# A four-layer graph network: the last layer's composition moved into PSUM, and empty second halves no longer gathered

## The chip, the cores and the metric

The kernel runs on one core of a Trainium2 chip. The metric is the device time of one execution in microseconds (us). Engines are named as in the profile: PE is TensorE (PEld its weight loads), DVE is VectorE, ACT is ScalarE, POOL is GpSimd and SP is SyncE; a name with a q is an engine's own instruction queue.

## The reference, cut to what matters

Four graph layers over 3125 nodes and 103125 edges, each behind a layer norm and a relu, and each added to x. The change touches the first layer (three hops) and the last:

```python
# layer 0, three times
h, t = agg[head], agg[tail]
att = sum((h @ q_w) * tanh(rel * t @ k_w), axis=1)
w = segment_softmax(att, head)
agg = segment_sum(w * rel * t, head) / count, normalised
# layer 3, once
comp = ent_emb[src] + rel_emb[rel_id]
score = sum(comp * ent_emb[dst], axis=-1)
norm = segment_softmax(score, dst)
neigh = segment_sum(comp * norm, dst)
return tanh(neigh @ neigh_w)
```

## The kernel before, in words

Nodes are sorted by degree and laid into 25 blocks of 128, one node to a partition. The edges of a block are laid out in slots: a body holds S = 8 slots for each of its 128 nodes, in two halves of H = 4 slots. A block has as many halves as its largest degree asks for, so its last body can have an empty second half. The plan in SBUF holds, for each block, the number of halves and the first body; with the reference's inputs the blocks have 15, 11, 11, then four times 10, six times 9, six times 8, four times 7 and two times 6 halves. That makes 116 bodies, and 13 blocks with an odd number of halves. Blank slots point at a blank row; the softmax gives them weight zero.

Two of the layers gather rows of a table in DRAM with one indirect DMA on POOL for each slot, 128 rows of 512 bytes at a time. Both use `PairStream`: `words` and `land` are double buffers, by the parity of the body. SP's `feed` loads a body's words, waits for the rows of each half (`rows_in`), passes them on (`rows_ready`, L877) and, after the first half of body n, passes the words of body n + 1 (`pass_words`, L864). POOL's `gather_all` waits for the words of body n and, for each half, for `rows_used`, then issues four gathers (L895); it does so for every body and for one blank body behind the last. So POOL gets the words of the next body only when the first half of the present one has landed.

In the first layer DVE makes a one-hot of the kinds (L1509, `kinds`), multiplies landed rows with relation rows (L1518), and sums and scores; PE and ACT work between. The first layer repeats this in three hops.

In the last layer (`composed_attention`), for body n inside the loop:

- DVE: `kinds(n + 3)` (L2359), `mark`, the eight score reductions of body n over `comp` in SBUF (L2403), the softmax steps of `soft.scores`, then for each half `compose(n + 1)` (L2379, landed rows plus the relation rows in PSUM) and `hots(n + 2)` (L2368, the one-hot for PE), then a wait for ACT's weighed rows and `soft.add` (L975 to L984).
- PE: `widen_kinds(n + 3)` (L2258, eight small matmuls that spread the kinds over the partitions), then `relations(n + 2)` (L2269), 48 bf16 matmuls for each half: 4 slots, 4 parts of the 474 relations, 3 bf16 terms.
- ACT: `move_line(n + 3)` (L2305: an activation table load, then a copy of 1024 columns), the exponentials (L960, L961) of body n, `weigh(n)` (L2317, eight), and last `keep(n + 1)` (L2312, two copies of 512 columns of `comp`).
- POOL: the gathers of body n + 2, which wait for `compose(n)` through `rows_used`.

One more place is read below for its durations alone: the graph convolution's second pass over the edges (L2046, `sums(1, ...)`), where TensorE multiplies f32 rows with 25 tiles of counts, six matmuls of 512 columns and one of 128 for each tile, 175 matmuls that the trace records as 350.

Each engine's order is the order of the code; there is no scheduler.

## Time and profile before

| | |
|---|---|
| median of 3 runs | 10402.22 us (10383.02 to 10405.49) |
| the profiled execution's own time | 10442.8 us |
| its span, first to last instruction | 10441.0 us |
| mean granted PE clock | 0.78 of full speed |
| busy share: PE, DVE, ACT, POOL | 65%, 73%, 56%, 66% |
| first layer, from its first one-hot to the end of hop three | 2142 to 5855 us |
| last layer, its loop over the bodies | 9013 to 10366 us |

The span is the time from the first instruction to the last on the core. The profiled execution is 40.6 us (0.4%) above the median of the timed runs. An engine's busy share is an average over stages with different limits, so the two touched stages are read apart.

### The profile page before, as it was taken

What the parts mean: (1) busy time and instruction counts of PE and PEld (TensorE: products, weight loads), DVE (VectorE), ACT (ScalarE), POOL (GpSimd) and SP (SyncE); (2) the same over time, 40 slices, a digit from 0 to 9 for tenths busy, and PEclk for the clock granted to TensorE, in tenths of its full rate; (3) what the DMA queues carried; (4) which work ended last, traced back from release to release, by engine and by line L of the source; (5) the groups of instructions that cost most, each with busy time, mean ns of one, the idle gap of its engine ahead of it and who ended that gap; (6) DMA issues with size and microseconds to landing.
All of it is one profiled execution on the core that took longest, in us unless ns stands there. A gap on an engine that the chain in (4) does not pass through costs nothing. (4 is left out here: it accounts for less than half of the span.)

```text
span 10441.0 us, 223670 instructions
## 1 busy us (share of the span) xinstructions
PE 6793.8 (65%) x64938; PEld 5513.0 (53%) x64939; DVE 7662.8 (73%) x21955; ACT 5833.8 (56%) x12496; POOL 6924.2 (66%) x5757
## 2 busy tenths in 40 slices
PE   3983974456665666656666487777777748466665
PEld 2883973345454455545555355555555523366655
DVE  9779764557777677767777699899989910577776
ACT  4224224446665566646666398889879900255544
POOL 0777764067776777767777489779869640566665
PEclk8555555677877788877878799999999979678777
DMA  0110119532322323223222211111111185222222
GB/s 23 54 43 22 57 38 139 184 48 53 53 53 46 51 53 53 52 45 51 53 53 53 44 51 57 51 46 57 57 39 57 57 140 208 47 47 47 46 45 44
DMA packets 421738, 630.49 MB, mean 60 GB/s; under 512 B 274855, under 2 KB 332033, under 8 KB 397929
## 3 DMA queue, kind: packets, MB, share of 16 engines
q0 software_dynamic: 192432, 385.10, 17.9%
q1 hardware_dynamic: 161808, 158.87, 5.9%
q10 hardware_dynamic: 67401, 85.32, 3.4%
q8 instruction: 50, 0.82, 0.0%
q14 instruction: 47, 0.39, 0.0%
HBM read 527.43 MB, written 103.02 MB: 60 GB/s over the span
## 5 line engine op out<-in xcount | busy, mean ns | idle before, releaser
L895 POOL DMA_INDIRECT l_land<-table,l_words x3744 | 3598.9, 961 | 1342.8 <-issue 1157.7
L1709 POOL DMA_INDIRECT ell<-gat_stage_pay,gat_stage_at x576 | 1675.0, 2908 | 175.5 <-issue 175.5
L1392 PE MATMUL left_product_ps<-k_w,messageT 128*128 128x128 f32 x5616 | 1046.7, 343 | 529.9 <-ACT messageT L1427 529.9
L1392 PEld LDWEIGHTS left_product_ps<-k_w,messageT 128*128 128x128 f32 x5616 | 883.0, 240 | 736.2 <-ACT messageT L1427 736.2
L2269 PE MATMUL rel_ps<-relation_parts,hot 128*128 128x128 bf16 x11328 | 823.1, 247 | 414.8 <-DVE hot L2368 414.8
L1806 ACT COPY gat_probT<-gat_ps 128x512 f32<-128x512 f32 (+1 forms) x2100 | 1018.7, 550 | 96.2 <-PE gat_ps L1749 83.4
L1386 PE MATMUL left_turned_ps<-ident,message 128*128 128x128 f32 x2808 | 563.1, 336 | 732.3 <-DVE message L1518 732.1
L244 POOL DMA_INDIRECT ell<-pay,position x816 | 840.2, 1030 | 292.5 <-issue 283.2
L2269 PEld LDWEIGHTS rel_ps<-relation_parts,hot 128*128 128x128 bf16 x11328 | 802.6, 114 | 436.4 <-DVE hot L2368 436.4
L1443 ACT ACTIVATE weighed<-kept,l_prob 128x128 f32 x2784 | 888.9, 391 | 59.1 <-ACT l_prob L961 59.0
L1386 PEld LDWEIGHTS left_turned_ps<-ident,message 128*128 128x128 f32 x2808 | 390.5, 174 | 832.6 <-DVE message L1518 829.4
L1749 PE MATMUL gat_ps<-ident,gat_logit 128*128 128x128 f32 x3750 | 600.7, 295 | 311.4 <-ACT gat_logit L1798 291.7
L295 PE MATMUL looked_ps<-count,loT_wide 128*128 (+1 forms) x3264 | 755.6, 384 | 48.4 <-issue 45.3
L1378 PE MATMUL rel_ps<-relation_parts,hotT 128*128 128x256 bf16 x4248 | 775.6, 334 | 2.0 <-ACT hotT L1422 2.0
L295 PEld LDWEIGHTS looked_ps<-count,loT_wide 128*128 128x128 f32 x3264 | 744.7, 333 | 57.2 <-issue 54.7
L1439 ACT ACTIVATE right<-left_product_ps 128x512 f32<-128x512 f32 x702 | 417.8, 595 | 636.8 <-DVE l_score L1579 363.6
L1755 PE MATMUL gat_ps<-gat_probT,h 128*32 128x128 f32 x15000 | 706.4, 282 | 2.4 <-issue 2.1
L1749 PE MATMUL gat_ps<-ident,work 128*128 128x128 f32 x3750 | 573.9, 284 | 180.3 <-ACT work L1798 159.9
L981 DVE TENSOR_REDUCE part<-weighed 128x128 f32<-128x1024 f32 x348 | 666.8, 1916 | 25.7
L1749 PEld LDWEIGHTS gat_ps<-ident,gat_logit 128*128 128x128 f32 x3750 | 430.1, 147 | 476.0 <-ACT gat_logit L1798 327.7
L353 ACT CAST loT_wide<-loT 128x512 f32<-128x512 bf16 x408 | 252.0, 618 | 700.9 <-PE looked_ps L299 675.0
L1579 DVE CUSTOM_DVE_ANT_0 product<-right,left_now 128x128 f32<-128x128 f32 x2784 | 623.1, 287 | 8.6
(334 smaller groups left out, 16136.3 us busy)
## 6 DMA issues: line engine op xcount, KB each, us to landing
gcn_edges<-counts SPq DMA_DIRECT2D x50, 1600.0 KB, 8.5
l_land<-table,l_words POOLq DMA_INDIRECT x3744
rows<-low_dram SPq DMA_DIRECT2D x34, 1536.0 KB
counts<-pair_turned_sb ACTq DMA_DIRECT2D x12, 3200.0 KB
logs<-pair_logs ACTq DMA_DIRECT2D x12, 3200.0 KB, 18.2
ell<-pay,position POOLq DMA_INDIRECT x816
ell<-gat_stage_pay,gat_stage_at POOLq DMA_INDIRECT x576
l_words<-ell SPq DMA_DIRECT2D x476, 8.0 KB
```

What stands on the lines that cost most here:

```text
L244: pool.indirect_dma_start(c.ells[0][:, :], bass.IndirectOffsetOnAxis(ap=position[:, 0, t:t + 1], axis=0), pay[:, t, :], None).then_inc(pla ...
L295: pe.matmul(looked_ps[r % HALVES][:, j, :], loT_wide[:, r % CAST, j, :], count[:, bass.ds(tile + j, 1), :].rearrange("p a n -> p (a n)"), ...
L895: pool.indirect_dma_start(self.land[:, p, s, :], None, table[:, :], bass.IndirectOffsetOnAxis(ap=self.words[:, p, s, 0:1], axis=0)).then_i ...
L1378: mm = pe.matmul(rel_ps[:, pair, :].rearrange("p s d -> p (s d)"), hotT[:, k * (H // 2) + j, :], parts[:, t, :, :].rearrange("p s d -> p ( ...
L1386: mm = pe.transpose(messageT_ps[:, k * H + j, :], message[:, k * H + j, :], c.ident[:, :])
L1392: mm = pe.matmul(right_ps[:, k * H + j, :], messageT[:, k, j, :], k_w[:, :], start=True, stop=True)
L1443: last = nc.scalar.activation(weighed[:, s, :], kept[:, bass.ds(n % 2, 1), s, :].rearrange("p a d -> p (a d)"), ACT.Copy, scale=soft.prob[ ...
L1709: pool.indirect_dma_start(c.ells[1][:, :], bass.IndirectOffsetOnAxis(ap=stage_at[n % 2][:, t:t + 1], axis=0), stage_pay[n % 2][:, t, :], N ...
L1749: mm = pe.transpose(ps[:, q % 4, r * P:(r + 1) * P], logit[t % 2][:, j * P:(j + 1) * P], c.ident[:, :])
L1755: mm = pe.matmul(ps[C * r:C * (r + 1), 4 + t % 2, 0:P], xs[:, 4 * q + r, t * C:(t + 1) * C], probT[:, q % 4 * 4 + r, :], start=(q == 0), s ...
L1806: nc.scalar.copy(probT[:, q % 4 * 4:q % 4 * 4 + rows_of(q), :].rearrange("p r d -> p (r d)"), ps[:, q % 4, 0:rows_of(q) * P]).then_inc(mov ...
L2269: mm = pe.matmul(rel_ps[:, k * H + s, :], hot[:, k, g, s, :], parts[:, g, t, :], start=(g == 0 and t == 0), stop=(g == PARTS - 1 and t == 2))
```

## The change

**The stream.** `gather_all` and `feed` now walk the plan block by block (`each_body`). POOL issues the four gathers of a second half only where the body has one, counted by `seconds`, whose own parity chooses the semaphore; it does not gather the blank body behind the last. SP waits for the second half only where there is one, and signals `rows_ready` in any case. The parity of a body is now told by two `If` blocks (`by_parity`) and no longer by an unrolled pair. The landing buffers' second halves are set to zero once for each layer. Two new functions, `read_plan` and `gather_by_plan`, are called by nothing.

**The last layer.** `comp` and `rel3_ps` are gone; two PSUM tiles `comp3_ps0` and `comp3_ps1` (two banks each) take turns by parity. For each half PE adds the landed rows with one f32 matmul of 512 columns against the identity, and the 48 relation matmuls accumulate on top. DVE's scores read PSUM; ACT's `keep` copies from PSUM and now stands before the exponentials; DVE's two additions are gone, and DVE's scores wait for ACT's copies of that body.

```diff
 class PairStream:
     def open(self, v):
+        self.nc.vector.memset(self.land[:, :, H:S, :], 0.0)
+        v.drain()
+    def each_body(self, eng, visit):
+        with eng.Fori(0, self.z.blocks) as b:
+            many, whole, first = self.block(eng, b)
+            seconds = self.second(eng, b)
+            with eng.Fori(0, many) as i:
+                visit(eng.snap((first + i).with_bounds(min_val=0, max_val=self.z.bodies - 1)), i < whole, seconds + i)
+
+    def by_parity(self, eng, n, visit):
+        with eng.If((n & 1) < 1):
+            visit(0)
+        with eng.If((n & 1) > 0):
+            visit(1)
 # feed, for each body
+            self.by_parity(sp, n, first_half)
+            self.pass_words(sp, base + n + 1)
+            s = hop * all_seconds + seconds
+            with sp.If(has_second):
+                self.by_parity(sp, sp.snap(s), lambda q: stand(sp, self.sp_turns, self.rows_in[q][1],
+                                                               (s >> 1) * (16 * H) + 16 * H))
+            sp.sem_inc(self.rows_ready[1], 1)
+            self.by_parity(sp, n, lambda p: go_on(n, p))
 # gather_all, for each body
+            def both(p):
+                stand(pool, self.turns, self.words_ready, hop * (bodies + 2) + n + 1)
+
+                stand(pool, self.turns, self.rows_used[0], hop * bodies + n + 1)
+                half(p, 0, self.rows_in[p][0])
+                with pool.If(has_second):
+                    stand(pool, self.turns, self.rows_used[1], hop * bodies + n + 1)
+                    self.by_parity(pool, pool.snap(s), lambda q: half(p, 1, self.rows_in[q][1]))
 # last layer, PE
+                    pe.wait_ge(stream.rows_ready[k], m + 1)
                     pe.wait_ge(hot_ready[k], m + 1)
-                    pe.wait_ge(comp_ready[k], m + 2)
+                    if not first:
+                        pe.wait_ge(scored, m + (-1))
+                        stand(pe, pe_turns, kept_ready[k], m + (-1))
+                    def into(p):
+                        pe.matmul(comp_ps[p][:, k * H:(k + 1) * H, :].rearrange("p s d -> p (s d)"), c.ident[:, :],
+                                  stream.landed(m, k).rearrange("p s d -> p (s d)"),
+                                  start=True, stop=False).then_inc(stream.rows_used[k], 1)
 # last layer, ACT's loop
                     move_line(i + 3)
+                    for k in range(HALVES):
+                        keep(act.snap(i + 1), k)
                     soft.exponentials(act, i)
                     act.wait_ge(soft.prob_ready, i + 1)
                     for k in range(HALVES):
                         weigh(i, k)
-                    for k in range(HALVES):
-                        keep(i + 1, k)
 # last layer, DVE
-                V.tensor_tensor(comp[:, half, :], stream.landed(n, k), rel_ps[:, half, :],
-                                ALU.add).then_inc(comp_ready[k], 1)
+                            last = V.tensor_tensor_reduce(product[:, s, :], comp_ps[p][:, s, :], h_now[:, :], op0=ALU.mult,
+                                                          op1=ALU.add, scale=1.0, scalar=0.0, accum_out=soft.score[:, s, :])
```

How the instructions stand. ACT in the last layer's loop, before: from the copy of the widened kinds to the first weighed slot.

```order
L2305 ACT_TABLE_LOAD
L2305 COPY kind_line<-line_ps 128x1024
L2287 ISA
L2287 DMA kind3<-ell1 128x16
L959 REGISTER_ALU
L960 ACTIVATE l3_keep<-l3_drop 128x1
L961 ACTIVATE l3_prob<-l3_score 128x8
L2317 ISA
L2317 ACTIVATE weighed3<-kept3,l3_prob 128x128
```

ACT with the change, from the first copy of a composed half (after the same table load, copy of kinds and DMA) to the exponentials. Of the four copies two run, by parity:

```order
L2400 COPY kept3<-comp3_ps0 128x512
L862 UNCONDITIONAL_BRANCH
L864 COMPARE_AND_BRANCH
L2400 COPY kept3<-comp3_ps1 128x512
L864 UNCONDITIONAL_BRANCH
L862 COMPARE_AND_BRANCH
L2400 COPY kept3<-comp3_ps0 128x512
L862 UNCONDITIONAL_BRANCH
L864 COMPARE_AND_BRANCH
L2400 COPY kept3<-comp3_ps1 128x512
L864 UNCONDITIONAL_BRANCH
L1033 ACTIVATE l3_keep<-l3_drop 128x1
```

The two copies of 512 columns stood behind the eight `weighed3` rows and now stand ahead of `l3_keep` and `l3_prob`.

PE in the last layer's loop, before: the widened kinds and both halves' relation matmuls.

```order
L2278 ISA
L2258 MATMUL line_ps<-ident_b,kind_b 128x128 x8
L2264 REGISTER_ALU
L2269 MATMUL rel3_ps<-relation_parts3,hot3 128x128 x96
L2278 REGISTER_ALU
L2278 COMPARE_AND_BRANCH
```

PE with the change, from the widened kinds to the first half's end; the second half repeats the pattern:

```order
L2333 MATMUL line_ps<-ident_b,kind_b 128x128 x8
L2339 REGISTER_ALU
L2342 REGISTER_ALU
L862 REGISTER_ALU x2
L862 COMPARE_AND_BRANCH
L2346 ISA
L2346 MATMUL comp3_ps0<-l3_land,ident 128x512
L2352 MATMUL comp3_ps0<-relation_parts3,hot3 128x128 x48
L862 UNCONDITIONAL_BRANCH
L864 COMPARE_AND_BRANCH
```

A 512-column f32 matmul with the identity stands ahead of each 48, and each half is inside a branch by parity.

POOL in the first layer, with the change: one body of even parity in the loop. Before, a body was two waits on semaphores and eight gathers in a row.

```order
L44 ISA x2
L917 DMA l0_land<-table,l0_words 128x128 x4
L929 REGISTER_ALU x2
L929 COMPARE_AND_BRANCH
L862 ISA
L862 REGISTER_ALU
L862 COMPARE_AND_BRANCH
L917 DMA l0_land<-table,l0_words 128x128 x4
L862 UNCONDITIONAL_BRANCH
L864 COMPARE_AND_BRANCH
L917 DMA l0_land<-table,l0_words 128x128 x4
L864 UNCONDITIONAL_BRANCH
```

The second four gathers stand inside two branches, and the block's two table words are read ahead of the loop.

## Rows read from the trace of the kernel before

**Rows 1.** Busy us by engine in two stretches, instructions in brackets, granted clock, DMA share, GB/s

```profile
2142.20:5855.00 3712.80, 2326.01 (x14191) 1863.61 (x14192) 2747.10 (x12158) 2289.26 (x5942) 2740.90 (x2853) 0.79 0.29 51
9012.80:10365.60 1352.80, 866.61 (x12016) 839.00 (x12016) 1066.20 (x4938) 687.31 (x1611) 890.72 (x926) 0.79 0.27 46
```

**Rows 2.** Groups by line, last layer's loop: busy, mean ns, idle before and releaser

```profile
L895 POOL DMA_INDIRECT l_land<-table,l_words x926 | 891.3, 963 | 454.0 <-issue 274.7 <-DVE comp L2379 170.0 <-SPq L864 9.2
...
L2403 DVE CUSTOM_DVE_ANT_0 l_product<-comp,h_now 128x128 f32<-128x128 f32 x920 | 204.7, 285 | 0.0
```

**Rows 3.** Timeline of two bodies, last layer: start, length, engine, line, idle before

```profile
9735.45 0.17 DVE L2359 TENSOR_SCALAR kind_b<-kind 128x8 bf16<-128x8 int32 x1 [0.85 <-issue]
...
9735.96 0.61 PE L2258 MATMUL line_ps<-ident_b,kind_b 128*128 128x128 bf16 x8
...
9740.54 8.08 PE L2269 MATMUL rel_ps<-relation_parts,hot 128*128 128x128 bf16 x96 [3.97 <-DVE hot L2368]
...
9745.85 0.17 DVE L2359 TENSOR_SCALAR kind_b<-kind 128x8 bf16<-128x8 int32 x1 [0.85 <-issue]
...
9748.45 0.61 PE L2258 MATMUL line_ps<-ident_b,kind_b 128*128 128x128 bf16 x8
...
9749.32 1.28 ACT L2305 ACT_TABLE_LOAD   x1 [6.34 <-issue]
...
9751.04 5.53 PE L2269 MATMUL rel_ps<-relation_parts,hot 128*128 128x128 bf16 x96 [1.97 <-DVE hot L2368]
...
9751.52 0.21 ACT L960 ACTIVATE l_keep<-l_drop 128x1 f32<-128x1 f32 x1
...
9754.35 1.12 ACT L2312 COPY kept<-comp 128x512 f32 x2
9754.55 0.15 DVE L975 COPY l_top_now<-l_top_new 128x1 f32<-128x1 f32 x1 [1.92 <-ACT weighed L2317]
...
9758.31 0.17 DVE L2359 TENSOR_SCALAR kind_b<-kind 128x8 bf16<-128x8 int32 x1 [0.85 <-issue]
```

**Rows 4.** Waits, last layer: total us, times, longest

```profile
ACT L2305 <- PE line_ps L2258: 586.1, 107, 7.6
```

**Rows 5.** Timeline of TensorE in the graph convolution

```profile
8731.61 136.53 PE L2046 MATMUL gcn_ps<-gcn_edges,work 128*128 128x512 f32 x350 [40.52 <-issue]
```

**Rows 6.** The same stretch, columns as in group 1

```profile
8732.00:8868.00 136.00, 136.00 (x350) 63.05 (x349) 0.00 (x0) 0.00 (x0) 0.00 (x0) 0.99 0.70 253
```

**Rows 7.** Groups by line, one hop of the first layer

```profile
L895 POOL DMA_INDIRECT l_land<-table,l_words x934 | 896.2, 960 | 291.7 <-issue 289.2 <-SPq L864 2.1 <-DVE message L1518 0.3
```

**Rows 8.** Waits, first layer's three hops

```profile
DVE hot L1509 <- SPq L864: 421.8, 273, 8.5
...
POOL l_land L895 <- DVE message L1518: 0.3, 1, 0.3
```

**Rows 9.** Timeline around one end of a half's gathers, first layer

```profile
2632.55 0.98 POOL L895 DMA_INDIRECT l_land<-table,l_words  x1 [0.30 <-issue]
...
2635.91 0.69 DVE L1509 TENSOR_TENSOR hot<-iota_row,l_words 128x512 bf16<-128x512 f32 x1 [1.36 <-SPq L864]
...
2638.97 0.94 POOL L895 DMA_INDIRECT l_land<-table,l_words  x1 [0.30 <-issue]
```

**Rows 10.** Timeline of a POOL wake, last layer

```profile
9703.58 0.69 DVE L2379 TENSOR_TENSOR comp<-l_land,rel_ps 128x512 f32<-128x512 f32 x1 [0.19 <-issue]
...
9705.06 1.07 POOL L895 DMA_INDIRECT l_land<-table,l_words  x1 [2.59 <-DVE comp L2379]
```

**Rows 11.** DVE's waits in a middle stretch of hop one

```profile
DVE hot L1509 <- SPq L864: 76.2, 61, 4.2
```

**Rows 12.** The same in its last stretch

```profile
DVE hot L1509 <- SPq L864: 9.5, 6, 4.5
```

**Rows 13.** Timeline of the last layer's start

```profile
9006.11 0.69 DVE L2379 TENSOR_TENSOR comp<-l_land,rel_ps 128x512 f32<-128x512 f32 x1 [27.34 <-SPq L877]
...
9017.83 0.32 DVE L2359 TENSOR_SCALAR kind_b<-kind 128x8 bf16<-128x8 int32 x1 [4.58 <-DMA kind<-ell]
```

More of the change, by code:

```diff
@@ L871, in feed, with go_on @@
         self.load_words(sp, 1, 1)
-        def step(n, j, p):
-            for h in range(HALVES):
-                stand(sp, self.sp_turns, self.rows_in[p][h],
-                      (hop * self.of_parity(bodies, p) + j) * (16 * H) + 16 * H)
-                sp.sem_inc(self.rows_ready[h], 1)
-                if not h:
-                    self.pass_words(sp, base + n + 1)
+        def go_on(n, p):
             if kinds_done:
@@ L885, in feed @@
+        self.each_body(sp, step)
+        for h in range(HALVES):
+            sp.sem_inc(self.rows_ready[h], 1)
+        self.pass_words(sp, base + bodies)
+        last = sp.snap(bodies + (-1))
+        self.by_parity(sp, last, lambda p: go_on(last, p))
         self.pass_words(sp, base + bodies + 1)
     def gather_all(self, pool, hop, bodies, table):
[L889 to L897 removed]
@@ L899, in gather_all, with half, step @@
-        self.in_pairs(pool, bodies, step)
+        all_seconds = self.all_second(pool)
+        def half(p, h, landed):
+            for s in range(h * H, (h + 1) * H):
+                pool.indirect_dma_start(
+                    self.land[:, p, s, :], None, table[:, :],
+                    bass.IndirectOffsetOnAxis(ap=self.words[:, p, s, 0:1], axis=0)).then_inc(landed, 16)
+        def step(n, has_second, seconds):
+            s = hop * all_seconds + seconds
+            def both(p):
[5 more added lines that the diff above has]
+                    self.by_parity(pool, pool.snap(s), lambda q: half(p, 1, self.rows_in[q][1]))
+            self.by_parity(pool, n, both)
@@ new lines, in gather_all, with read_plan, gather_by_plan, half @@
+        self.each_body(pool, step)
+    def read_plan(self, pool):
+        return [pool.value_load(self.plan[0:1, b:b + 1], min_val=1, max_val=(1 << 31) - 1)
+                for b in range(self.z.blocks)]
+    def gather_by_plan(self, pool, hop, bodies, table, words):
+        most = self.z.bodies
+        def half(p, h, landed):
+            for s in range(h * H, (h + 1) * H):
+                pool.indirect_dma_start(
+                    self.land[:, p, s, :], None, table[:, :],
+                    bass.IndirectOffsetOnAxis(ap=self.words[:, p, s, 0:1], axis=0)).then_inc(landed, 16)
+        seconds = hop * self.all_second(pool)
+        for b, word in enumerate(words):
+            halves = word & ((1 << HALF_BITS) - 1)
+            many = pool.snap(((halves + 1) >> 1).with_bounds(min_val=1, max_val=most))
+            whole = pool.snap((halves >> 1).with_bounds(min_val=0, max_val=most))
+            first = pool.snap((word >> HALF_BITS).with_bounds(min_val=0, max_val=most))
+            s0 = pool.snap(seconds)
+            with pool.Fori(0, many) as i:
+                n = pool.snap(first + i)
+                def both(p):
+                    stand(pool, self.turns, self.words_ready, hop * (bodies + 2) + n + 1)
+                    stand(pool, self.turns, self.rows_used[0], hop * bodies + n + 1)
+                    half(p, 0, self.rows_in[p][0])
+                    with pool.If(i < whole):
+                        stand(pool, self.turns, self.rows_used[1], hop * bodies + n + 1)
+                        self.by_parity(pool, pool.snap(s0 + i), lambda q: half(p, 1, self.rows_in[q][1]))
+                self.by_parity(pool, n, both)
+            seconds = s0 + whole
```

85 lines of the change are left out of this document (41 added, 44 removed).

## The prediction

> **What bounds the kernel now.** Only two stages change, so I read each by itself: first the busy time of every engine in each stretch, then the groups by line, then the waits, and last the timeline of single bodies. The last layer's waits are small pieces that repeat, and only the timeline shows how they join.
>
> The first layer's three hops take 3713 us and POOL is busy for 2741 of them, no more than DVE [rows 1]. But a gather of 960 ns is followed by idle time that nothing in the profile ends ("issue"). With it one gather costs (896.2 + 291.7) / 934 = 1.27 us, and eight make 10.2 us, the whole pace of a body; POOL waited for DVE once, for 0.3 us [rows 7, 8]. DVE waits for the words 273 times, 421.8 us in all [rows 8]. So this layer is bound by POOL's gathers.
>
> The last layer is not. Its 116 bodies take 1352.8 us [rows 1], 11.66 each, and POOL waits for DVE's additions for 170 us [rows 2]. The timeline shows a short body of 10.40 us (K = 9735.45 to 9745.85, K being the start of the kinds) and a long one of 12.46 us (to 9758.31) [rows 3]. Both end by the same chain: line matmuls, 0.87 us later ACT's table load, 2.20 later the exponentials, 3.03 later DVE's L975, 3.76 later the next K, together 9.86 us. In the short body the line matmuls start at K + 0.51, and 0.51 + 9.86 = 10.37. In the long one they start at K + 2.60, because the relation matmuls of the body before began at its K + 5.09 and took 8.08 us; 2.60 + 9.86 = 12.46. The next batch took 5.53 us, was over before the next K, and so the next body is short again [rows 3]. ACT's waits agree: 586.1 us for the line matmuls, 107 times [rows 4]. What a body waits for last is PE's batch and then ACT's chain. DVE's 74 to 79% busy is no bound.
>
> **The stream, first layer.** 13 blocks have an odd number of halves; each drops four gathers in each hop: 39 bodies, 4 × 1.27 = 5.08 us of POOL's time each [rows 7]. Not all of it is won. SP passes the next body's words only when the first half has landed. In a whole body four more gathers cover that, in an odd one nothing does. From the start of a first half's last gather to the release of DVE, which SP's same turn brings, is 2635.91 − 2632.55 = 3.36 us [rows 9]. POOL then needs about 0.8 us to wake, as behind DVE's addition (9704.27 to 9705.06) [rows 10]. So 4.2 us pass where 6.42 (to 2638.97) pass now [rows 9], and an odd body wins 2.2 us, not 5.08.
>
> DVE must be able to follow. In the middle of a hop it waits 76.2 us over 61 waits, 1.25 each; in the last stretch, where the blocks of 7 halves lie, 9.5 us over 810 and 220 us [rows 11, 12]. So nine blocks win 2.2 and the four of 7 halves about 0.4: 3 × (19.8 + 1.6) = 64, rounded down for a first body here and there: **−62 us**. Bounds: −85 if DVE keeps up everywhere; −20 if each saved gap returns as a DVE wait. The new `If`s, table words and branches of POOL I cost at nothing: its sequencer runs ahead, since the 0.30 us before a gather is the same at a new body [rows 9]. If that cover failed, see the last rival. The blank body's gathers stood behind the last real ones and ended nothing; the memset is below 2 us. Second halves dropped in the last layer win nothing, since POOL waits there [rows 2].
>
> **The last layer.** Three edits touch the 9.86 us chain or the batch ahead of it.
>
> PE gets two f32 matmuls of 512 columns. The nearest row is the graph convolution: 136.53 us at a granted clock of 0.99 for 25 tiles, 5.46 us for six matmuls of 512 and one of 128 columns, each recorded twice [rows 5, 6]; 5.46 / 6.25 = 0.87 us for a matmul of 512. Two take 1.7 us at 2.4 GHz, and twice that, 3.4 us, at 1.2 GHz. The first batch of a pair takes 8.08 us against the other's 5.53 and so begins at the lower level; the mean granted clock is 0.79 [rows 1, 3]. I take +2.15 us: one half's at 2.4 GHz with part of the other's at 1.2. The start of the batch stays at K + 5.09: the one-hot comes 0.6 us sooner without the first addition, and three more waits and a branch stand before the batch.
>
> The Trainium skill ("TensorE: Matmul & The Clock Gate", section "Back-to-back issue gap") gives N/2.4 + 2.5 ns for an isolated matmul, 0.22 us for 512 columns. The rows have four times that for f32. By the page two would cost 0.43 us, a pair +1.55 and the kernel about 10447.
>
> ACT's two copies of 512 columns, 1.12 us [rows 3], stood behind the weighed rows, in ACT's idle time, and now stand ahead of the exponentials: **+1.12** on the chain in every body. They could hide only if DVE's scores came later than they; they don't, since the exponentials now follow the table load and the copies of kinds by ACT's own work.
>
> DVE's two additions (2 × 0.69 us [rows 10]) are gone. They lie between the scores and the one-hots, while ACT weighs; L975 ended a wait of 1.92 us for ACT [rows 3], and this wait grows by the 1.38 us. The gain is nothing. The scores now read PSUM; 285 ns each [rows 2] is from SBUF, and this trace has no such read from PSUM. Half that again on eight is 1.1 us, still less than the 1.38 + 1.92 us of room. The Trainium skill ("VectorE: DVE Perf Modes", section "⚠️ The TRN2 errata — SBUF-src ops pay a fixed extra latency per instruction") has 120 fixed cycles for a PSUM source against 58, by an estimate 65 ns each and 0.5 us for eight; no row shows it, and the room would take it.
>
> So a pair goes from 22.86 to 22.86 + 2.15 + 1.12 = 26.1 us, +3.27. The blocks' bodies (8; 6, 6; four of 5; six of 5; six of 4; four of 4; two of 3) make 52 pairs and 12 single short ones: 52 × 3.27 = 170, 12 × 1.12 = 13. At the start PE's first two batches, now run while the table is being written, must wait for landed rows. The first compose is at 9006.11 and the loop's K at 9017.83 [rows 13]; two batches of 5.53 + 1.7 us behind the first rows, less the second's overlap with the kinds, end about 9020 + 10: **+13**. In sum **+196**. Bounds: +100, if the f32 matmuls take 1.7, half the copies hide and the batch starts 0.6 sooner (pair +1.7: 52 × 1.7 = 88, and 12 for the rest); +260, if they run at 1.2 GHz (pair +4.5: 234 and 26).
>
> **Sum.** −62 + 196 = +134. The profiled execution took 10442.8, so 10577; the runs' median is 40.6 below it: **10536 us**.
>
> **The rivals.** Besides the forecast (0.72):
>
> PE keeps 2.4 GHz, *faster* (0.09). With more work PE's idle gaps shrink; if its first batch ran at 2.4 GHz too it would take 5.53 + 1.7 = 7.2 us, less than today's 8.08. A pair is then 5.09 − 0.17 + 7.2 + 10.98 = 23.1, +0.2; 10 + 13 + 13 − 62 = −26, 10376 us. It decides if the longer first batch takes under 7.7 us (pair +0.7), where the sum is zero. Against it: PE still has its idle of 4 us in front of that batch [rows 3].
>
> The copies and the batch lie off the path, *faster* (0.05): if bodies then waited for DVE alone, every pair would be two short bodies, 20.8 for 22.86; −107 − 62 = −169, 10233 us. Against it speak the 586.1 us [rows 4].
>
> There is no stall in an odd body, *slower all the same* (0.07): nine blocks win the whole 5.08 us, 3 × (9 × 5.08 + 1.6) = 142, and −142 + 196 = +54, 10456 us. It needs the release of the words to come 3 us sooner behind a first half than rows 9 have it.
>
> POOL's control comes out in the open, *slower still* (0.07): `by_parity` inside `If` inside two loops is some 0.5 us for each of 350 bodies in the first layer, +175, hence 10711 us. Against it: the even 0.30 us [rows 9]. That dropped halves save nothing at all is the −20 end.
>
> **The numbers.** ±0.2% of 10402 is 21 us, about what a measurement of this kernel can tell from no change. The likeliest case gives 10536. The ends of the unknown costs, −85 + 100 and −20 + 260, give 10417 and 10642; both ends together are rare, so the range is 10440 to 10640. It holds nearly all of the forecast's 0.72 and of the third rival's 0.07, and leaves the rest out. Faster: the second rival's 0.05 and 0.06 of the first's 0.09. Same: the other 0.03 of the first, 0.02 from the third's lower half, 0.02 from the low ends of the forecast: 0.07. Slower: the rest, 0.82.
>
> **What would show it.** In the changed profile: the first layer 60 us shorter, with waits of POOL for SP's words in 39 bodies, about 3 us each; none would mean the stall is not there. In the last layer, about 1550 us: two f32 records of 0.43 us or more ahead of each half; batches of 10 and 7 us in turn; short bodies of 11.5 us; the exponentials 3.3 us behind the table load where they are 2.2 now; the wait of L975 for ACT up from 1.92 to above 3 us. I am wrong if PE's granted clock there is above 0.9, if bodies of the last layer stay near 11.7 us, or if the first layer gets longer.

## The result, and the profile after

| | before | with the change |
|---|---|---|
| median of 4 runs | 10399.54 us (10383.02 to 10405.49) | 10605.12 us (10601.62 to 10606.37) |
| profiled execution, its span | 10442.8, 10441.0 us | 10606.37, 10604.6 us |
| first layer, first one-hot to last | 3717.6 us (2134.4 to 5852.0) | 3699.4 us (2102.1 to 5801.5) |
| last layer, first kinds to last K | 1391.8 us (8973.8 to 10365.6) | 1612.7 us (8912.4 to 10525.1) |
| of that the loop, first K to last K | 1347.8 us (from 9017.8) | 1558.4 us (from 8966.7) |

The ratio is 1.0202, 95% interval 1.0189 to 1.0214: slower by 2%, about 206 us. The forecast was 10536 us in a range to 10640, so direction and range held and the median fell 69 us above it. The table already says where: between these two profiles the first layer gave 18 us and not 62, and the last layer took 221 and not 196. The two spans differ by 164 us only, since the profiled execution of before was 32 us longer ahead of the first layer and 11 us longer between it and the last, where the only new instruction is a memset of 0.91 us for each layer; without these 43 us the stages add up to about the 206 of the medians.

The 18 us lean on one profile of each kernel. From first one-hot to last, the three profiles below that have the old stream take 3717.6, 3711.6 and 3710.0 us; the changed kernel, in two profiles, and its six variants with the same new stream take 3696.9 to 3710.5, 3702 on average. By these the new stream is worth some 11 us.

Two stretches of the changed kernel, by engine, columns as in [rows 1]: the first layer, and the last layer's loop.

```profile
2102.10:5801.50 3699.40, 2307.75 (x14183) 1852.73 (x14184) 2741.86 (x12151) 2282.33 (x5932) 2587.12 (x2678) 0.80 0.21 48
8966.70:10525.10 1558.40, 1079.19 (x12420) 878.63 (x12420) 950.48 (x4702) 679.98 (x1610) 807.83 (x854) 0.83 0.17 37
```

POOL's busy time in the first layer fell by 154 us against [rows 1], mostly its 39 × 4 gathers, while the stretch fell by 18. In the last layer PE's busy time rose from 867 to 1079 us and the granted clock from 0.79 to 0.83.

The last layer's loop by groups (busy, mean ns, then idle before and its releasers), where [rows 2] answer:

```profile
L2346 PE MATMUL comp_ps<-l_land,ident 128*128 x460 | 315.4, 773 | 376.2 <-issue 203.6 <-DVE hot L2459 121.4 <-ACT kept L2400 49.7
...
L2470 DVE CUSTOM_DVE_ANT_0 l_product<-comp_ps,h_now 128x128 f32<-128x128 f32 x920 | 203.4, 286 | 42.5 <-issue 42.4
```

The f32 matmuls appear as two records for each half, which overlap: 315.4 us for 230 halves, 1.37 us a half, 2.7 us a body. A score of DVE from PSUM takes 286 ns, against 285 from SBUF. But ahead of the eight scores DVE now stands idle, 42.5 us in all, where [rows 2] have 0.0: they wait for ACT's copies and stand behind a branch by parity.

Two bodies of the last layer, the counterpart of [rows 3] (start, length, engine, line, idle before). K is again the start of a body's kinds on DVE:

```profile
9733.35 0.19 DVE L2450 TENSOR_SCALAR kind_b<-kind 128x8 bf16<-128x8 int32 x1 [0.85 <-issue]
...
9733.60 0.62 PE L2333 MATMUL line_ps<-ident_b,kind_b 128*128 128x128 bf16 x8 [1.75 <-DVE kind_b L2450]
...
9734.16 0.29 DVE L2470 CUSTOM_DVE_ANT_0 l_product<-comp_ps,h_now 128x128 f32<-128x128 f32 x1 [0.50 <-issue]
...
9737.21 2.19 DVE L2459 TENSOR_SCALAR hot<-kind_line,kind_of 128x512 bf16 x8 [0.18 <-issue]
...
9739.46 2.07 PE L2346 MATMUL comp_ps<-l_land,ident 128*128 x2 [5.24 <-issue]
...
9741.33 4.18 PE L2352 MATMUL comp_ps<-relation_parts,hot 128*128 128x128 bf16 x48
...
9744.44 0.17 DVE L2450 TENSOR_SCALAR kind_b<-kind 128x8 bf16<-128x8 int32 x1 [0.86 <-issue]
...
9745.34 1.08 PE L2346 MATMUL comp_ps<-l_land,ident 128*128 x2
...
9746.25 2.84 PE L2352 MATMUL comp_ps<-relation_parts,hot 128*128 128x128 bf16 x48
...
9748.93 0.61 PE L2333 MATMUL line_ps<-ident_b,kind_b 128*128 128x128 bf16 x8
9749.80 1.28 ACT L2391 ACT_TABLE_LOAD   x1 [9.23 <-PE line_ps L2333]
...
9752.00 1.08 ACT L2400 COPY kept<-comp_ps 128x512 f32<-128x512 f32 x2
...
9752.95 0.23 ACT L1033 ACTIVATE l_keep<-l_drop 128x1 f32<-128x1 f32 x1
...
9756.00 0.15 DVE L1048 COPY l_top_now<-l_top_new 128x1 f32<-128x1 f32 x1 [5.50 <-ACT weighed L2406]
...
9759.81 0.17 DVE L2450 TENSOR_SCALAR kind_b<-kind 128x8 bf16<-128x8 int32 x1 [0.85 <-issue]
```

Read it by the prediction's steps. K = 9733.35, and the batch begins at 9739.46, K + 6.11, where it was K + 5.09. From there to the next line matmuls, 9748.93, pass 9.47 us; it was 7.91. The f32 matmuls in it take 2.07 us for the first half and 1.08 for the second. From the line matmuls to the next K (9759.81) pass 10.88 us; it was 9.86, and the new part is the row of ACT's two copies, 9752.00, between the table load and the exponentials. The pair is 26.46 us for 22.86. Not every pair is like this one: in one block of five bodies the kinds begin 12.94, 13.76, 13.57 and 11.87 us apart.

Why the batch begins later can be read too. Before, in the body of [rows 3] that begins at K = 9735.45, DVE's first score and its first one-hots were

```profile
9735.66 0.31 DVE L2403 CUSTOM_DVE_ANT_0 l_product<-comp,h_now 128x128 f32<-128x128 f32 x1
...
9739.34 1.14 DVE L2368 TENSOR_SCALAR hot<-kind_line,kind_of 128x512 bf16 x4
```

The first score began at K + 0.21 and now begins at K + 0.81 (9734.16). So the one-hots, with the first addition gone from in front of them, begin at K + 3.86 (9737.21) where they began at K + 3.89: nothing is won. And from their start to PE's batch pass 2.25 us, where 1.20 passed (9739.34 to 9740.54). In the changed loop the first score begins mostly at K + 0.6 to 0.8.

The waits of the last layer (total us, times, longest), where [rows 4] answer:

```profile
ACT L2391 <- PE line_ps L2333: 848.7, 114, 10.0
...
DVE l_top_now L1048 <- ACT weighed L2406: 337.5, 113, 5.5
```

ACT waits for the line matmuls 848.7 us, where it was 586.1: the same wait still ends last.

The first layer's waits, before and after. The kernel before, DVE's own:

```profile
DVE l_top_now L975 <- ACT weighed L1443: 143.1, 171, 3.1
```

With the change:

```profile
DVE l_top_now L1048 <- ACT weighed L1516: 231.2, 231, 2.8
DVE hot L1582 <- SPq L873: 175.4, 85, 9.5
DVE hot L1582 <- issue: 135.9, 266, 0.7
```

DVE's wait for words fell from 421.8 to 175.4 us. Half a microsecond at each of 266 one-hots is put down to "issue" (135.9 us; it was 41.4 at 78 of them). And DVE's wait for ACT's weighed rows rose from 143.1 to 231.2 us. One wait takes the place of the other.

DVE has also become slower in a place that the diff doesn't touch, the maximum of a body's scores. Its group in the first layer, before and after:

```profile
L950 DVE TENSOR_REDUCE l_top_body<-l_score 128x1 f32<-128x8 f32 x347 | 55.8, 161 | 25.6
...
L1023 DVE TENSOR_REDUCE l_top_body<-l_score 128x1 f32<-128x8 f32 x347 | 55.9, 161 | 69.2 <-issue 69.2
```

The idle time before it went from 0.07 to 0.20 us a body, 44 us in three hops. It is the same in every profile with the new stream and in none with the old. Why is not shown, nor how much of the 44 us ends on the path.

### The profile page after: what moved, and what is told of

Same layout as the page of the kernel before. It is cut to its first block and busy times, and to the rows that moved or that the text cites. A ratio compares the mean times of both kernels' runs of the same rounds, so it can differ in the third digit from the quotient of the medians.

```text
span 10604.6 us, 240300 instructions
## 1 busy us (share of the span) xinstructions
PE 6982.9 (66%) x65410; PEld 5536.6 (52%) x65411; DVE 7547.1 (71%) x21723; ACT 5824.5 (55%) x12496; POOL 6692.4 (63%) x5518
## 5 line engine op out<-in xcount | busy, mean ns | idle before, releaser
L917 POOL DMA_INDIRECT l_land<-table,l_words x3504 | 3368.4, 961 | 1713.6 <-issue 1251.7
L2352 PEld LDWEIGHTS comp_ps<-relation_parts,hot 128*128 128x128 bf16 x11328 | 765.0, 108 | 178.7 <-issue 178.7
L2352 PE MATMUL comp_ps<-relation_parts,hot 128*128 128x128 bf16 x11328 | 780.1, 237 | 0.0
```

Of the source, the lines that this page charges most:

```text
L917: pool.indirect_dma_start(self.land[:, p, s, :], None, table[:, :], bass.IndirectOffsetOnAxis(ap=self.words[:, p, s, 0:1], axis=0)).then_i ...
L2352: mm = pe.matmul(comp_ps[p][:, k * H + s, :], hot[:, k, g, s, :], parts[:, g, t, :], start=False, stop=(s == H - 1 and g == PARTS - 1 and ...
```

## The experiments

Each edit is against the changed kernel unless it says otherwise. In what follows "hops" are the first layer's three stretches from first to last one-hot (1195.0, 1193.2, 1194.6 us before; 1188.9, 1186.3, 1187.3 with the change), and "loop" is the last layer's as in the table above. A ratio is to the kernel before, timed beside the variant.

**Stream alone.** `composed_attention` as before, on the new stream; no other edit.

> The new stream with the last layer as it was before. If the two parts of the change are independent (theory: the last layer costs about +222 us, the first layer gives about -17), this is 15 to 25 us faster than before, near 10380 us, with the last layer's loop at 1348 us again. Rival (the last layer's loss is partly the stream's, because SP's and POOL's longer control delays landed rows there): the last layer's loop is longer than before by tens of us and the kernel is slower than before.

10409.99 us against 10414.86, ratio 0.9994 (0.9985 to 1.0003): not to be told from no change, and not the 15 to 25 us. In the profile the loop is 1348.0 us, as before, and the hops are 1186.1, 1186.7 and 1187.8. So this profile has 19 us of the first layer, and the timed runs show some 6, with an interval that goes to 16. The rival is out: the stream costs the last layer nothing.

**Last layer alone.** The new `composed_attention` on the old stream (with `by_parity` added to the class).

> The old stream with the new last layer. Independent parts: +215 to +225 us on before, about 10620 us, the last layer's loop near 1558 us. Rival (stream and layer interact): the loop is clearly shorter than 1558 us with the old stream.

10642.21 us, ratio 1.0234 (1.0206 to 1.0262), loop 1563.8 us. The whole loss is here, and it is the same on either stream. The changed kernel itself, run once more:

> The changed kernel once more, unedited, beside the others on the same chip: +200 us on before, loop 1558 us, and the hops 1187 us. It is there so that the reorderings are compared with it in the same job.

10629.04 us against 10413.59, ratio 1.0208 (1.0191 to 1.0224), loop 1560.7, hops 1188.7, 1186.8, 1188.1. The loop repeats to 3 us, so the loops below can be compared.

**The copies behind the weighed rows.**

```diff
                     move_line(i + 3)
-                    for k in range(HALVES):
-                        keep(act.snap(i + 1), k)
                     soft.exponentials(act, i)
                     act.wait_ge(soft.prob_ready, i + 1)
                     for k in range(HALVES):
                         weigh(i, k)
+                    for k in range(HALVES):
+                        keep(act.snap(i + 1), k)
```

> The changed kernel with ACT's two copies behind the weighed rows again, everything else as changed. Theory (the copies lie on the chain from the table load to the next body): a body's chain from line matmuls to the next K falls by 1.0 us, a pair by 1.0 and a single short body by 0.7: 52 x 1.0 + 12 x 0.7 = 60 us less, about 10545 us. Rival (the copies are covered, since PE's batch sets the pace): below 15 us of gain, and ACT's wait for the line matmuls grows by what it wins. A second rival: the copies now end after DVE wants to score the next body, so that DVE waits for them, and nothing or little is won.

Ratio 1.0136 (1.0121 to 1.0152), loop 1478.8 us: 80 us less, more than the 60. Its timeline:

```profile
9740.73 0.61 PE L2333 MATMUL line_ps<-ident_b,kind_b 128*128 128x128 bf16 x8
...
9741.59 1.28 ACT L2391 ACT_TABLE_LOAD   x1 [9.29 <-PE line_ps L2333]
...
9743.79 0.21 ACT L1033 ACTIVATE l_keep<-l_drop 128x1 f32<-128x1 f32 x1
...
9746.62 1.04 ACT L2400 COPY kept<-comp_ps 128x512 f32<-128x512 f32 x2
...
9750.59 0.17 DVE L2450 TENSOR_SCALAR kind_b<-kind 128x8 bf16<-128x8 int32 x1 [0.85 <-issue]
```

The table load to the exponentials is 2.20 us again, as in [rows 3], and from the line matmuls to the next K 9.86. The copies (9746.62) run while DVE adds. They are hidden there, and the second rival, that DVE would wait for them, is out. By the starts of the kinds, 40 of the 80 us lie inside the blocks, less than the expectation's 60, and 40 in the last bodies of the 24 blocks that another follows (from 16.2 to 14.6 us each), which the expectation had taken for ordinary ones.

**The last wait inside the branch.**

```diff
-                    pe.wait_ge(stream.rows_ready[k], m + 1)
-                    pe.wait_ge(hot_ready[k], m + 1)
-                    if not first:
+                    if first:
+                        pe.wait_ge(stream.rows_ready[k], m + 1)
+                        pe.wait_ge(hot_ready[k], m + 1)
+                    else:
                         pe.wait_ge(scored, m + (-1))
                         stand(pe, pe_turns, kept_ready[k], m + (-1))
                     def into(p):
+                        if not first:
+                            pe.wait_ge(stream.rows_ready[k], m + 1)
+                            pe.wait_ge(hot_ready[k], m + 1)
                         pe.matmul(comp_ps[p][:, k * H:(k + 1) * H, :].rearrange("p s d -> p (s d)"), c.ident[:, :],
```

> The changed kernel with PE's waits for the landed rows and the one-hot moved inside the branch on parity, directly ahead of the f32 matmul: the same instructions, but the wait that ends last now comes last. Theory (1.0 us of PE's control between the one-hot and the first matmul delays the batch, in the chain of each pair): the batch starts 0.8 to 1.0 us earlier after K, 52 x 0.9 = 47 us less, about 10558 us. Rival (something else ends last there, the landed rows or ACT's copies): no gain, within 10 us of 10605.

Ratio 1.0161 (1.0146 to 1.0177), loop 1519.8 us: 39 less. The batch's row in its timeline, behind the kinds of that body:

```profile
9746.91 0.17 DVE L2454 TENSOR_SCALAR kind_b<-kind 128x8 bf16<-128x8 int32 x1 [0.85 <-issue]
...
9750.77 2.19 DVE L2463 TENSOR_SCALAR hot<-kind_line,kind_of 128x512 bf16 x8 [0.18 <-issue]
...
9752.19 2.07 PE L2350 MATMUL comp_ps<-l_land,ident 128*128 x2 [4.43 <-DVE hot L2463]
```

The batch begins at K + 5.28 (it was K + 6.11), and its releaser is now DVE's one-hot, where the changed kernel had "issue" (9739.46 above). The one-hots begin 1.42 us before the batch here and 2.25 us there: 0.83 us of PE's control had stood between a semaphore that was up and the matmul. Moving it gave 39 us and not 47.

**Without the f32 matmuls.** The landed rows are not added, so the output lacks them; the waits stay.

```diff
-                        pe.matmul(comp_ps[p][:, k * H:(k + 1) * H, :].rearrange("p s d -> p (s d)"), c.ident[:, :],
-                                  stream.landed(m, k).rearrange("p s d -> p (s d)"),
-                                  start=True, stop=False).then_inc(stream.rows_used[k], 1)
                         for s in range(H):
                             for g in range(PARTS):
                                 for t in range(3):
                                     mm = pe.matmul(comp_ps[p][:, k * H + s, :], hot[:, k, g, s, :], parts[:, g, t, :],
-                                                   start=False, stop=(s == H - 1 and g == PARTS - 1 and t == 2))
+                                                   start=(g == 0 and t == 0), stop=(g == PARTS - 1 and t == 2))
+                                    if s == 0 and g == 0 and t == 0:
+                                        mm.then_inc(stream.rows_used[k], 1)
```

> The changed kernel without the two f32 matmuls of 512 columns; the landed rows are not added, the first relation matmul of each half frees the landing buffer, all waits stay. Theory (the two matmuls lengthen the first batch of each pair by 1.56 us beyond today's order of things, the rest of the loss is the copies and PE's control): the last layer's loop is 52 x 1.56 = 81 us shorter, near 1477 us instead of 1558. Rival (PE's clock gives the work back: fewer columns, lower granted clock): under 40 us shorter and a lower granted clock in the loop. Second rival (the wait for landed rows, not the matmul, sets the start): unchanged.

Ratio 1.0116 (1.0087 to 1.0146), loop 1455.5 us: 103 less, where 81 was expected.

```profile
9015.20:10470.70 1455.50, 924.27 (x11960) 895.61 (x11960) 945.25 (x4702) 680.40 (x1610) 809.72 (x855) 0.77 0.18 40
```

PE is busy 924 us, 155 less than with the change, at a granted clock of 0.77 for 0.83. So the clock does follow the work, as the rival said: the 11040 relation matmuls take 858.6 us where they took 760.7 with the f32 matmuls among them. But the loop is 103 us shorter even so, and not under 40. The three parts, taken away one at a time, gave 80, 39 and 103 us, in sum 222, against a loss of the loop of 211. They account for the loss, though no run takes all three away at once; that they overshoot by 11 shows that they are not quite independent.

**Words passed early.** SP passes the next body's words before it waits for the first half.

```diff
+            self.pass_words(sp, base + n + 1)
             self.by_parity(sp, n, first_half)
-            self.pass_words(sp, base + n + 1)
```

> The changed kernel with SP passing the next body's words before it waits for the first half of the present one, in both layers. The prediction's theory (in a body without a second half POOL stands still because the words come late, and that costs time): the idle behind odd bodies falls from 4 us to under 1, and the three hops, 1187 us each now, become 15 us or more shorter each. Rival (DVE's loop with PE and ACT has its own pace of some 49.9 us for five bodies, and POOL's pause is slack): the pauses vanish or move, the hops stay within 3 us of 1187.

Hops 1186.4, 1185.8, 1184.7: 1.9 us less each on average, ratio of the kernel 1.0204 (1.0177 to 1.0231), as the changed one. The 1.9 us are no more than the hops differ by between kernels with the same first layer (1185.0 to 1192.0). The pause behind an odd body is there in both. First the changed kernel, one of POOL's gathers (start, length, idle before):

```profile
3819.71 0.94 POOL L917 DMA_INDIRECT l_land<-table,l_words  x1 [3.05 <-issue]
```

And with the words passed early:

```profile
3873.23 0.94 POOL L917 DMA_INDIRECT l_land<-table,l_words  x1 [1.40 <-DVE message L1591]
...
3881.17 0.94 POOL L917 DMA_INDIRECT l_land<-table,l_words  x1 [3.23 <-issue]
```

The pause has moved and split: one of 1.40 us now waits for DVE's `message`, which POOL hardly ever waited for in [rows 8], and one of 3.23 us remains. So the edit shortened the stall and did not remove it, and nothing clear was gained.

**Few gathers.** One gather in place of four in each second half; three quarters of those rows are not fetched.

```diff
-            for s in range(h * H, (h + 1) * H):
+            for s in range(h * H, (h + 1) * H if not h else H + 1):
...
-                                                               (s >> 1) * (16 * H) + 16 * H))
+                                                               (s >> 1) * 16 + 16))
```

> The changed kernel with one gather in place of four in each second half (the rest of those rows is not fetched), in both layers: POOL needs 5 x 1.25 = 6.3 us for a body in place of 10. Rival of before (DVE's loop is the next bound right below POOL's): the hops stay near 1180, at most 10 us below 1187, and DVE's waits for words fall to nearly none while those for ACT's weighed rows grow. The prediction's theory (POOL's gathers set the pace, DVE has over 1 us a body in reserve): the hops fall by 30 us or more each. The last layer's loop should not move (1558 us): POOL waits there.

Ratio 1.0155 (1.0128 to 1.0182). Hops 1174.6, 1174.2, 1173.3, some 13 us below the change; loop 1553.3. DVE's and POOL's waits in the first layer:

```profile
POOL l_land L917 <- issue: 1579.9, 1609, 5.7
...
DVE l_top_now L1048 <- ACT weighed L1516: 276.6, 271, 2.8
POOL l_land L917 <- DVE message L1591: 266.9, 92, 5.6
```

POOL had 3 gathers less in nearly every body and stood idle for over 1800 us. Still a hop lost 1% only, and DVE's wait for ACT's weighed rows went on rising, 143 to 231 to 277 us. Against before a hop lost some 20 us, 60 in all.

Where in a hop they lie can be read from DVE's L1048 (L975 before), which runs once a body. The first block of a hop has eight bodies; mean of three hops, us:

| | first one-hot to the ninth L1048 | from there to the last one-hot |
|---|---|---|
| before | 119.2 | 1075.1 |
| with the change | 118.8 | 1068.7 |
| few gathers | 106.1 | 1067.9 |

So 13 of the 20 us lie in the first block, which the change leaves as it was. Behind it, in 108 of 116 bodies, the change took 6 us, and with a great part of POOL's work gone there is 1 us more: there the changed kernel is already at a pace that POOL doesn't set. This is the rival's case, though the hops fell by 13 us and not by 10 at most.

**The line copy behind.** The old last layer on the new stream. ACT's copy of the widened kinds goes to the body's end, and with `late=True` the load of the next kinds is taken out of `move_line` and stands by itself, ahead of the kept copies. The exponential of one column, `warm`, takes the table load off the way of the real ones.

```diff
                 with act.Fori(0, all_bodies) as i:
-                    move_line(i + 3)
+                    nc.scalar.activation(warm[:, :], c.ident[:, 0:1], ACT.Exp)
                     soft.exponentials(act, i)
                     act.wait_ge(soft.prob_ready, i + 1)
                     for k in range(HALVES):
                         weigh(i, k)
+                    act.wait_ge(kind_ready, i + 4)
+                    load_kinds(i + 4)
                     for k in range(HALVES):
                         keep(i + 1, k)
+                    move_line(i + 3, late=True)
```

> The new stream with the old last layer, and in it ACT's copy of the widened kinds moved from the head of a body to its end, behind the weighed rows and the kept copies, with the load of kinds ahead of those and a tiny exponential at the head of the body that takes the table load. Theory (each long body is long because ACT's exponentials stand behind the line matmuls, which stand behind PE's batch): every body becomes a short one of about 10.4 us, 52 x 2.06 = 107 us less in a loop of 1348; the kernel near 10300 us, faster than both. Rival (the widened kinds then come too late for the one-hots, or kinds land too late): the loop is within 30 us of 1348 or longer, and DVE waits for ACT's line or for the kinds.

10336.06 us against 10420.66, ratio 0.9923 (0.9901 to 0.9945): faster than both kernels. Loop 1270.0 us, 78 less than before; hops 1192.0, 1190.7, 1190.8. Two bodies in a row:

```profile
9705.35 0.17 DVE L2437 TENSOR_SCALAR kind_b<-kind 128x8 bf16<-128x8 int32 x1 [0.49 <-issue]
...
9708.49 0.20 ACT L1033 ACTIVATE l_keep<-l_drop 128x1 f32<-128x1 f32 x1 [6.88 <-DVE l_score L1028]
...
9710.45 8.15 PE L2343 MATMUL rel_ps<-relation_parts,hot 128*128 128x128 bf16 x96 [4.24 <-DVE hot L2446]
...
9715.76 0.17 DVE L2437 TENSOR_SCALAR kind_b<-kind 128x8 bf16<-128x8 int32 x1 [0.85 <-issue]
...
9715.98 0.29 DVE L2481 CUSTOM_DVE_ANT_0 l_product<-comp,h_now 128x128 f32<-128x128 f32 x1
...
9718.43 0.61 PE L2332 MATMUL line_ps<-ident_b,kind_b 128*128 128x128 bf16 x8
...
9718.88 0.20 ACT L1033 ACTIVATE l_keep<-l_drop 128x1 f32<-128x1 f32 x1 [4.02 <-DVE l_score L1028]
...
9722.48 0.14 DVE L1048 COPY l_top_now<-l_top_new 128x1 f32<-128x1 f32 x1
...
9726.24 0.17 DVE L2437 TENSOR_SCALAR kind_b<-kind 128x8 bf16<-128x8 int32 x1 [0.85 <-issue]
```

The batch of 8.15 us still pushes the next line matmuls to 9718.43, 2.67 us behind K = 9715.76. But the exponentials no longer stand behind them: they come at K + 3.12 (9718.88), released by DVE's scores, and both bodies are short, 10.41 and 10.48 us. The 107 us expected was too much because not every long body was 12.46 us; the first one of a block was 11.5.

On the old stream the same edit was timed as well.

> The kernel before with ACT's copy of the widened kinds at the end of a body, as in the version on the new stream, but with the old stream. Theory (the gain of that version is all in the last layer): 78 us less than before, the loop near 1270 us, hops 1194 us; the new stream is worth another 6 to 20 us on top. Rival (POOL, which then has to fetch both halves of every body, comes near the bound at 10.2 us a body): the loop is 20 us or more longer than on the new stream.

10340.13 us against 10413.59, ratio 0.9931 (0.9917 to 0.9944), loop 1274.8, hops 1192.4, 1191.7, 1191.3. The gain is all in the last layer, and the new stream adds nothing that these intervals can tell; the three hops differ by 2 us in all from those of the same last layer on the new stream.

**All of it in the changed kernel.** The two reorderings of the changed kernel and the line copy behind, together.

> The changed kernel with three reorderings at once: PE's last wait inside the branch, ACT's kept copies and ACT's copy of the widened kinds behind the weighed rows, a tiny exponential at the head of the body for the table load. Theory (with the line matmuls off the chain PE's longer batches are covered, and DVE is freed of its two additions): a body falls below the 10.45 us of the version with the old last layer, to POOL's pace of 8 x 1.25 = 10.0 for a whole body or below, loop 1200 to 1240 us, kernel near 10260 us. Rival (PE's batch with the f32 matmuls, about 10 us with its control, or the loop through PSUM now sets the pace): bodies above 10.45 us, loop above 1270 us, slower than the version with the old last layer.

10351.67 us against 10413.59, ratio 0.9940 (0.9926 to 0.9953), loop 1274.6 us. So the changed kernel, reordered, is faster than before, and no better than the old last layer with one reordering. One body:

```profile
9705.81 0.17 DVE L2459 TENSOR_SCALAR kind_b<-kind 128x8 bf16<-128x8 int32 x1 [0.85 <-issue]
...
9706.41 0.29 DVE L2479 CUSTOM_DVE_ANT_0 l_product<-comp_ps,h_now 128x128 f32<-128x128 f32 x1 [0.29 <-issue]
...
9709.32 0.20 ACT L1033 ACTIVATE l_keep<-l_drop 128x1 f32<-128x1 f32 x1 [4.01 <-DVE l_score L1028]
...
9710.98 1.26 ACT L2412 ACTIVATE weighed<-kept,l_prob 128x128 f32 x4
...
9712.34 0.15 DVE L1048 COPY l_top_now<-l_top_new 128x1 f32<-128x1 f32 x1 [0.46 <-issue]
```

And its loop, columns as in [rows 1]:

```profile
9003.20:10277.80 1274.60, 997.10 (x12385) 819.24 (x12386) 961.05 (x4702) 701.12 (x1727) 809.53 (x854) 0.91 0.21 45
```

PE's longer batches are covered and the granted clock is 0.91. But the bodies are 10.3 to 10.5 us, not 10.0. Here DVE reaches L1048 at K + 6.53 (9712.34) and has waited 0.46 us on the way, ACT's weighed rows having ended at 9710.98 + 1.26 = 9712.24. With the additions it came there without a wait at K + 6.72 (9722.48 in the two bodies of the line copy behind, K = 9715.76). Of the 1.38 us that DVE was freed of, 0.2 arrive. Two things take the rest. The exponentials, which wait for the scores, begin at K + 3.51 (9709.32) where they began at K + 3.12, since the first score begins at K + 0.60 (9706.41) where it began at K + 0.22 (9715.98): 0.39 us of DVE's own waits and branch. And from the exponentials to L1048 pass 3.02 us, which is ACT's exponentials and weighing, where DVE's own work took 3.60: the path goes by ACT as soon as DVE's work is shorter. By an estimate from these rows, without the 0.39 us a body would take some 10.0 us, which is what the theory had; no run has tried it. So neither expectation held: the pace is the old one.

## Why the prediction was right, and where it was short

**The last layer's chain: right, with one term that failed.** The steps it rested on are in the timeline above. The f32 matmuls were put at +2.15 us for a pair and took 1.56 on the path. From its first record to the relation matmuls the first half's took 1.87 us (9739.46 to 9741.33) and the second's 0.91 (9745.34 to 9746.25), close to the 1.74 and 0.87 of [rows 5, 6]; but more of the batch ran at 2.4 GHz: the mean granted clock from its start to the line matmuls was 0.75, and 0.66 before. The copies were put at +1.12 and took 1.02. The start of the batch was put at zero and took +1.02: that is the term that failed. The prediction set 0.6 us of gain against "three more waits and a branch" and called it even, without a row for either. The gain did not come, since DVE's scores now begin 0.6 us later, a cost for which the prediction had no term; and PE's control took 1.05 us, of which the move of the last wait behind the branch gave 0.83 back. Together 3.60 us for a pair where 3.27 was forecast. That the two are so close is partly luck: the f32 term was 0.59 us too large and the start 1.02 too small.

The step from a pair to the loop was rougher than the pair. The prediction took 52 pairs at 22.86 us, but the first long body of a block took 11.5 us and not 12.46. Of the loop's 211 us, 164 lie inside the blocks and 47 in their last bodies (14.3 us became 16.2), which the prediction didn't set apart. 52 × 3.60 = 187 us holds only as far as the pair shown is typical. Taking out single parts bears out all three terms: 103, 80 and 39 us. The start-up was right: 44.0 became 54.3 us from the first kinds to the first K, +10 for +13. It is still 52.8 us without the f32 matmuls, so they are little of it; that the rest is the wait for landed rows, as the prediction had it, fits and was not tested by itself.

**What was put at nothing.** The dropped additions gained nothing in the changed kernel, as forecast: DVE's wait for ACT at L1048 grew instead, to 5.50 us in the long body where it was 1.92. A score from PSUM takes 1 ns more, as good as nothing; what costs is the 0.4 to 0.6 us ahead of the first one. The Trainium skill ("VectorE: DVE Perf Modes", section "⚠️ The TRN2 errata — SBUF-src ops pay a fixed extra latency per instruction") has 120 fixed cycles for a PSUM source against 58; the trace doesn't agree, with 286 against 285 ns for this instruction. The Trainium skill's 0.22 us for an isolated matmul of 512 columns ("TensorE: Matmul & The Clock Gate", section "Back-to-back issue gap") is not what an f32 one costs here: 0.91 us from its first record to the next matmul at the upper level.

**The stream: direction right, size more than three times too large.** The failed step is DVE's reserve. The prediction read 1.25 us for each wait of DVE for words as room, in nine of thirteen blocks [rows 11]. But when words come sooner DVE meets its wait for ACT's weighed rows: by the starts of L975 and L1048 a block of 9 halves went from 50.9 to 50.2 us on average, not to 48.7, and with few gathers it is at 50.2 too. So 0.7 us of the 2.2 was won, and no more was there. The blocks without an odd half were put at nothing and got longer: those of 10 halves from 50.2 to 50.8 us, those of 8 from 40.5 to 40.7; the 0.13 us a body that DVE now idles at L1023 is a likely cause, not a tested one. Even with three of the four gathers of each second half gone the three hops are only 60 us shorter than before, 39 of them in their first blocks.

The pause that the prediction saw behind odd bodies is there, and as often as forecast: 39 idle stretches of POOL from 2.8 to 4.9 us, 4.1 on average, none of that size before. It was named as what limits the gain. It isn't, since the blocks are no shorter when POOL has time to spare.

**The base.** The 40.6 us between the profiled execution of before and the median fit the 43 us by which its untouched stages were longer than the changed kernel's; with one profile of each that is no proof. The changed kernel's profiled execution is within 1.3 us of its median. Of the 72 us by which +206 passes +134, 44 are the stream's, 25 the last layer's, and 3 the rest's, by these two profiles.

**The rivals.** PE at the upper clock all the time: the granted clock did rise, 0.79 to 0.83, but the first batch of a pair began at the lower level still. A pace by DVE alone: it came about only with the line copy moved. No stall in an odd body: the 39 stalls are there; out. POOL's control in the open: the gathers stay 0.30 us apart at a new body; out.

**The signs.** Of what the prediction said would show it, these came: the loop near 1550 us (1558), batches of 10 and 7 us in turn (9.47 and 7.39), the exponentials 3.3 us behind the table load (3.15), and DVE's wait for ACT above 3 us in the long body. The short bodies took 11.1 us for 11.5, and the first layer's 60 us did not come.

## What to carry to other kernels

Work moved from an engine that waits to an engine that is waited for lengthens the path (by 1.56 us for two f32 matmuls, by 1.02 for two copies), and what it frees is worth nothing until the wait it stood beside is gone. Before counting on an engine's idle time, take the work of the engine it waits for nearly away and see how far the stretch falls, and in which part of it: here it was 60 us where the waits said 420, and 39 of the 60 lay in the first block of each hop, which the change left as it was. Where a copy stands at the head of an in-order queue and waits for a long batch on another engine, everything behind it inherits that wait; moving that one copy took 78 us from the old loop, where the whole change added 211.

## What was not expected of the hardware

On PE, an engine's own control (a few waits, register operations and two branches) shows in full when the last wait stands ahead of the branch: 1.05 us more from the one-hots to the batch, 0.83 of it gone when the wait stands behind. On DVE the waits and the branch ahead of the scores cost 0.4 to 0.6 us a body. On POOL the control of a new body doesn't show: the gathers stay 0.30 us apart.

DVE's idle time ahead of an instruction that nobody touched went from 0.07 to 0.20 us a body in the first layer, with the new stream alone.

The granted clock follows the load of the same loop: 0.77 without the f32 matmuls, 0.79 before, 0.83 with the change, 0.86 with the copies behind, and 0.91 with all three reorderings, where the loop is shortest for the same work.
